# A vision tower on one core: GLA operands zeroed earlier and two tiles' products moved, shared-expert units of 144 and 384 columns, expert routing issued in three pieces

## What is computed

```python
h = _L0_tok_ref(L0_tok_log_dt, L0_tok_Lambda, x, 512)
h = jnp.concatenate([jnp.broadcast_to(cls_tok, (h.shape[0], 1, h.shape[2])), h], axis=1)
h = h + _L0_attn_ref(_layernorm(h), ...)   # gated linear scans, both directions
h = h + _L0_ffn_ref(_layernorm(h), ...)    # 8 experts, top 2, F = 256; shared expert, 512 wide
h = h + _L1_attn_ref(_layernorm(h), ...)   # GLA
h = h + _L1_ffn_ref(_layernorm(h), ...)    # 8 experts, top 2, F = 352; shared expert, 1408 wide
```

```python
q = silu(x @ Wq.T) * SCALE;  k = sigmoid(x @ Wk.T);  g = log_sigmoid(-k)
S = exp(g_t)[:, :, None] * S + k_t[:, :, None] * v_t[:, None, :];  o_t = q_t @ S     # v = x
go = o @ Wog.T + x @ Wig.T
out = o * rsqrt(mean(o*o) + EPS) * g_weight * go * sigmoid(go)
```

## Time and profile before

| | us |
|---|---|
| median of 3 runs (1746.93 to 1756.14) | 1748.59 |
| the profiled execution, its own time | 1747.31 |
| its span in the profile | 1745.5 |
| PE (TensorE) busy | 1483.2 (85%) |
| DVE (VectorE) busy | 795.7 (46%) |
| ACT (ScalarE) busy | 311.7 (18%) |
| mean granted TensorE clock | 0.956 of 2.4 GHz |

### The profile page before, as it was taken

The page is one execution under the profiler, slowest core; times in us unless marked ns, Lnnn a source line. Parts: engine busy times, 40 slices in busy tenths (PEclk is TensorE's granted clock), DMA queues, the critical chain, the costliest instruction groups (busy, mean ns, idle before and its releaser), DMA issues.

```text
span 1745.5 us, 19077 instructions
## 1 busy us (share of the span) xinstructions
PE 1483.2 (85%) x6021; PEld 1017.9 (58%) x6022; DVE 795.7 (46%) x1658; ACT 311.7 (18%) x575; POOL 381.1 (22%) x302
## 2 busy tenths in 40 slices
PE   0394748999899997259996899999999999999994
PEld 0393325888444443127775688888888755666652
DVE  7885487554222222832546655545555412222221
ACT  1022113211111111232222211111211111111110
POOL 0471320700244443001111160000000023333321
PEclk9999879999999999589998999999999999999997
DMA  2374005001855455300000611000000294333334
GB/s 50 67 127 101 0 24 200 20 31 49 310 94 96 84 85 107 115 1 0 1 1 25 227 32 37 18 18 18 18 29 8 88 357 77 61 65 66 66 60 121
DMA packets 73761, 128.86 MB, mean 74 GB/s; under 512 B 28784, under 2 KB 32752, under 8 KB 71280
## 3 DMA queue, kind: packets, MB, share of 16 engines
q1 hardware_dynamic: 53616, 86.20, 15.8%
q0 software_dynamic: 20096, 42.02, 13.3%
HBM read 81.86 MB, written 47.50 MB: 74 GB/s over the span
## 4 chain that ended last, share of the span: by engine, by line
PE 82%; DVE 10%; DMA 2%; issue 2%; ACT 1%; SPq 1%; POOL 0%; POOLq 0%; DVEq 0%; ACTq 0%
PE ps L1297 21%; PE ps L1234 11%; PE ps L1346 11%; PE ps L1363 10%; PE ps L1342 8%; PE ps L1707 6%; PE ps L402 3%; PE ps L1331 2%; DVE held L455 2%; PE ps L511 1%; DMA h_rows<-moe_scratch 1%; PE ps L1354 1%; PE ps L730 1%; PE ps L1679 1%; PE ps L731 1%
## 5 line engine op out<-in xcount | busy, mean ns | idle before, releaser
L1297 PE MATMUL ps<-moe_rounded 128*128 128x512 f32 (+1 forms) x1800 | 406.2, 369 | 0.0
L1297 PEld LDWEIGHTS ps<-moe_rounded 128*128 128x128 f32 x1800 | 316.1, 190 | 66.7
L1074 DVE SCALAR_TENSOR_TENSOR held<-ps,moe_scratch,held 128x512 f32<-128x512 f32 (+1 forms) x255 | 183.8, 746 | 221.9 <-PE ps L1234 221.9
L1234 PE MATMUL ps<-moe_rounded 128*128 128x512 f32 (+3 forms) x885 | 232.9, 392 | 16.3 <-DVE moe_rounded L1058 15.0
L1149 POOL DMA_INDIRECT moe_scratch<-xn_rows,moe_scratch x80 | 78.1, 976 | 597.0 <-PE ps L1331 584.7
L1346 PE MATMUL ps<-moe_experts,moe_scratch 128*128 x640 | 196.1, 460 | 1.3 <-ACT moe_scratch L1215 0.9
L1234 PEld LDWEIGHTS ps<-moe_rounded 128*128 128x128 f32 (+2 forms) x885 | 150.3, 172 | 64.9 <-DVE moe_rounded L1058 16.7
L1363 PE MATMUL ps<-moe_experts,moe_scratch 128*128 (+1 forms) x400 | 185.3, 594 | 2.6 <-DVE moe_scratch L1097 2.3
L1158 POOL DMA_INDIRECT h_rows<-moe_scratch x80 | 126.6, 1582 | 235.0 <-DVE moe_scratch L1090 158.3
L1084 DVE TENSOR_TENSOR moe_scratch<-moe_scratch,ps 128x256 f32<-128x256 f32 (+1 forms) x80 | 37.7, 471 | 275.6 <-ACT moe_scratch L1221 275.6
L1346 PEld LDWEIGHTS ps<-moe_experts,moe_scratch 128*128 128x128 f32 x640 | 118.7, 190 | 60.8 <-issue 1.8
(11 more groups left out here) (273 smaller groups left out, 1420.4 us busy)
## 6 DMA issues: line engine op xcount, KB each, us to landing
moe_experts<-in_ffn_gate_up SPq DMA_DIRECT2D x8, 1408.0 KB, 15.8
xn_rows<-moe_xn SPq DMA_DIRECT2D x2, 4096.0 KB, 13.2
moe_experts<-in_ffn_gate_up SPq DMA_DIRECT2D x8, 1024.0 KB, 12.3
moe_experts<-in_ffn_down SPq DMA_DIRECT2D x16, 512.0 KB, 14.4
h_rows<-held SPq DMA_DIRECT2D x8, 1024.0 KB, 4.1
moe_scratch<-in_ffn_sh_gate_up SPq DMA_DIRECT2D x15, 512.0 KB, 3.5
out<-h_rows SPq DMA_DIRECT2D x4, 1032.0 KB, 10.0
tokens<-sb SPq DMA_DIRECT2D x64, 64.0 KB, 2.3
```

The costliest lines, as they stand in the source:

```text
L1074: v.scalar_tensor_tensor(out=hb[0:rows, t, :], in0=ps[0:rows, 4 + r % 3, :], scalar=sg[0:rows, t:t + 1], in1=hb[0:rows, t, :], op0=ALU.mul ...
L1234: mm = t.matmul(out, lhs(k, x), rhs(k, y), start=(k == 0 and i == 0), stop=(k == ks - 1 and i == 2))
L1297: mm = t.matmul(unit_banks(unit)[j], weights(k, x, j), xT[y][:, k, unit_cols(unit)[0]], start=(k == 0 and i == 0), stop=(k == KD - 1 and i ...
```

## The change

It does five things.

1. Shared expert: unit 0 is the last 144 columns (tile 15 and the class tile), unit 4 is 384 columns (tiles 12 to 14). The downs of tiles 15 and 16 come with those of unit 1, as fifth and sixth in rank. So six downs stand in unit 2 and three (of unit 4) in the next block's unit 1.
2. Routing: VectorE enters the first block at once, and does the routing in three pieces: `segments` after the multiplication of unit 1, `slots_of` after the low part of unit 1, `tile_experts` after the first two adds. The third down of the first block waits for a new count, `RANKED`.
3. GLA: the zeroing stands before VectorE's first wait for `hb`.
4. GLA, VectorE: the low part of `xc3` before the split of the output weights; `low_part(0)` before the first operation of the decay chain, `low_part(1)` between scan and reciprocal, `cls_xw` behind the reciprocal. On ScalarE `high_part(1)` stands before `xw_out(0)`, and `xw_out(1)` before the copy of the class scores.
5. GLA, TensorE: `gate_x(0)`, `xw_of(1)` and `gate_x(1)` stand ahead of `attend(0)`, after `xw_of(0)`.

```diff
+RC = P + NB
...
-    hid, hidc = r.take(2, 2, QC), r.take(2, NB)
+    hid, hidc = r.take(2, 2, QC), r.take(2, RC)
...
+    DIFFERENCES, CHOICES, RANKED, ROUTED = 1, 2, 3, 4
...
-        return (slice(NCOL, NTOK), NB) if m == 0 else (slice((m - 1) * QC, m * QC), QC)
+        if m == 0:
+            return slice(NTOK - RC, NTOK)
+        return slice((m - 1) * QC, min(m * QC, NTOK - RC))
...
-        tiles = list(range(4 * (m - 1), 4 * m)) + ([NB] if m == 1 else [])
+        tiles = list(range(4 * (m - 1), min(4 * m, NB - 1))) + ([NB - 1, NB] if m == 1 else [])
...
-        return 4 if tile == NB else tile + (tile > 3)
+        return tile - NB + 5 if tile >= NB - 1 else tile + 2 * (tile > 3)
...
         if m == 0:
-            return ps[:, 7, 0:NB], ps[:, 7, NB:2 * NB]
-        p = 2 * ((m - 1) % 2)
-        return ps[:, p, :], ps[:, p + 1, :]
+            return ps[:, 7, 0:RC], ps[:, 7, RC:2 * RC]
+        p, w = 2 * ((m - 1) % 2), unit_width(m)
+        return ps[:, p, 0:w], ps[:, p + 1, 0:w]
+
+    def unit_width(m):
+        return unit_cols(m).stop - unit_cols(m).start
...
-        for j, oh in enumerate((oh0, oh1)):
...
-        c.link(v.tensor_tensor(cmp, bc(iot.unsqueeze(2), 2, NE), bc(incl.unsqueeze(1), 1, NTILE), ALU.is_ge))
-        c.link(v.tensor_reduce(etab, cmp, AX.X, ALU.add))
-        v.tensor_scalar(eti, etab, float(NE - 1), None, ALU.min).then_inc(rt, 1)
-        norm.closed(c)
-        v.wait_ge(sgm, 2)
+
+        def segments():
+
+            c.link(v.memset(anew, 1.0))
+            c.put(v.memset(anew[:, :, 0], 0.0))
+            c.link(v.memset(one8, 1.0))
+            v.wait_ge(rp, T + 1)
+            c.link(v.tensor_tensor_scan(upto.rearrange("p e t -> p (e t)"), anew.rearrange("p e t -> p (e t)"), ps[:, 6, 256:256 + T * NE], 0.0, ALU.mult, ALU.add))
+            c.link(v.tensor_scalar(cni, upto[:, :, T - 1], float(P - 1), None, ALU.add))
+            c.link(v.tensor_tensor(upto, upto, in_tile, ALU.subtract))
+            v.tensor_tensor(mm8, ps[:, 6, 64:64 + T * NE].rearrange("p (t e) -> p t e", e=NE), upto.rearrange("p e t -> p t e"), ALU.add).then_inc(rt, 1)
+            c.link(v.tensor_scalar(cni, cni, 7, None, ALU.arith_shift_right))
+            c.link(v.tensor_copy(cnt, cni))
+            c.link(v.tensor_tensor_scan(incl, one8, cnt, 0.0, ALU.mult, ALU.add))
+
...
+            c.link(v.tensor_tensor(base, incl, cnt, ALU.subtract))
+            c.link(v.tensor_scalar(base, base, float(P), None, ALU.mult))
+            v.wait_ge(rt, RANKED)
+            c.link(v.tensor_tensor(mm8, mm8, bc(base.unsqueeze(1), 1, T), ALU.add))
+            for j, oh in enumerate((oh0, oh1)):
+                c.link(v.tensor_tensor(t8, oh, mm8, ALU.mult))
+                c.link(v.tensor_reduce(m1, t8, AX.X, ALU.add))
+                c.link(v.tensor_copy(slot_u[:, j], m1))
...
+            v.wait_ge(sgm, 2)
+
+        def tile_experts():
+
+            c.link(v.tensor_tensor(cmp, bc(iot.unsqueeze(2), 2, NE), bc(incl.unsqueeze(1), 1, NTILE), ALU.is_ge))
+            c.link(v.tensor_reduce(etab, cmp, AX.X, ALU.add))
+            v.tensor_scalar(eti, etab, float(NE - 1), None, ALU.min).then_inc(rt, 1)
+            norm.closed(c)
...
+        ROUTING = {("mul", 1): segments, ("lo", 1): slots_of, ("early", 1): tile_experts}
...
+                if is_first(b) and (what, m) in ROUTING:
+                    ROUTING[what, m]()
...
-                        s.wait_ge(dn, b * T + (unit_rank(unit_tiles(m - 2)[3]) + 1 if m >= 3 else (5 - T, 13 - T, 0)[m]))
+                        s.wait_ge(dn, b * T + (unit_rank(unit_tiles(m - 2)[3]) + 1 if m >= 3 else (6 - T, 14 - T, 0)[m]))
...
-            m = 0 if tile == NB else tile // 4 + 1
-            j = 0 if tile == NB else tile % 4
+            m, j = (0, tile - NB + 1) if tile >= NB - 1 else (tile // 4 + 1, tile % 4)
...
+            if is_first(b) and r == 2:
+                t.wait_ge(rt, RANKED)
             if r >= 3:
                 t.wait_ge(acc, b * T + r - 2)
...
+        c.put(v.memset(ss, 1.0))
+        c.link(v.memset(bv, 0.0))
+        c.put(v.memset(bv[:, :, 0], 1.0))
+        c.put(v.memset(kcz, 0.0))
+        c.put(v.memset(own, 0.0))
+        v.memset(xc3[0:ROWS3].bitcast(F32), 0.0).then_inc(c3, 1)
+        v.memset(xwc3[0:ROWS3].bitcast(F32), 0.0).then_inc(c3, 1)
+        c.wait()
+        for j in range(3):
+            c.put(v.tensor_copy(own[KH * j:KH * j + NB], ident[KH * j:KH * j + NB, KH * j:KH * j + NB]))
         for tiles in GROUPS:
             for n in tiles:
...
-        c.put(v.memset(ss, 1.0))
-        c.link(v.memset(bv, 0.0))
...
+        v.wait_ge(c3, 4)
+        v.tensor_tensor(xc3[KH:KH + NB], xn[0:NB, NB, :], xc3[0:NB], ALU.subtract).then_inc(c3, 1)
         v.wait_ge(wsp, 2)
         for w, to in ((wog, wo), (wig, wi)):
             v.tensor_tensor(to[:, 1], w, to[:, 0], ALU.subtract).then_inc(wsp, 1)
-        v.wait_ge(c3, 4)
-        v.wait_ge(xr, 1)
-        v.tensor_tensor(xc3[KH:KH + NB], xn[0:NB, NB, :], xc3[0:NB], ALU.subtract).then_inc(c3, 1)
...
+        low_part(0)
         v.wait_ge(bnd, 4 * NG + 1)
         v.scalar_tensor_tensor(out=qr, in0=qr, scalar=SILU_SCALE, in1=sq, op0=ALU.mult, op1=ALU.mult).then_inc(qkr, 1)
...
         c.link(v.tensor_tensor_scan(F(pv), F(av), F(bv), 0.0, ALU.mult, ALU.add))
+        low_part(1)
         c.link(v.reciprocal(F(av), F(pv)))
+        cls_xw()
         v.wait_ge(qkr, 1)
         v.tensor_tensor(qr, qr, pv, ALU.mult).then_inc(qkr, 1)
...
-        low_part(0)
-        cls_xw()
-        low_part(1)
...
         high_part(0)
+        high_part(1)
         xw_out(0)
-        high_part(1)
+        xw_out(1)
...
-            if j + 1 < T:
+            if 1 <= j and j + 1 < T:
                 xw_out(j + 1)
...
         xw_of(0)
+        gate_x(0)
+        xw_of(1)
+        gate_x(1)
         attend(0)
         cls_scores()
...
-            gate_x(j)
-            if j + 1 < T:
+            if j >= 2:
+                gate_x(j)
+            if 1 <= j and j + 1 < T:
                 xw_of(j + 1)
             outs(j)
```

More of the change, by code:

```diff
@@ L882, in sync @@
         for q in range(NQ):
-            sp.wait_ge(acc, (NSH - 1) * T + unit_rank(4 * q + 3) + 1)
+            sp.wait_ge(acc, (NSH - 1) * T + max(unit_rank(t) for t in range(4 * q, 4 * q + 4)) + 1)
             sp.dma_start(hd_rows[1:SEQ, 4 * q:4 * q + 4], hb[:, 4 * q:4 * q + 4, :]).then_inc(hst, 16)
@@ L1027, in vector @@
[L1027 to L1033, removed]
-        c.link(v.tensor_tensor(mm8, ps[:, 6, 64:64 + T * NE].rearrange("p (t e) -> p t e", e=NE), upto.rearrange("p e t -> p t e"), ALU.add))
@@ L1296, in block @@
                             for unit in units:
-                                mm = t.matmul(unit_banks(unit)[j], weights(k, x, j), xT[y][:, k, unit_cols(unit)[0]],
+                                mm = t.matmul(unit_banks(unit)[j], weights(k, x, j), xT[y][:, k, unit_cols(unit)],
                                               start=(k == 0 and i == 0), stop=(k == KD - 1 and i == 2))
@@ L1458, in vector @@
         v.wait_ge(xr, 1)
-        c.put(v.memset(ss, 1.0))
-        c.link(v.memset(bv, 0.0))
-        c.put(v.memset(bv[:, :, 0], 1.0))
-        c.put(v.memset(kcz, 0.0))
-        c.put(v.memset(own, 0.0))
-        v.memset(xc3[0:ROWS3].bitcast(F32), 0.0).then_inc(c3, 1)
-        v.memset(xwc3[0:ROWS3].bitcast(F32), 0.0).then_inc(c3, 1)
-        c.wait()
-        for j in range(3):
-            c.put(v.tensor_copy(own[KH * j:KH * j + NB], ident[KH * j:KH * j + NB, KH * j:KH * j + NB]))
+        v.wait_ge(c3, 4)
+        v.tensor_tensor(xc3[KH:KH + NB], xn[0:NB, NB, :], xc3[0:NB], ALU.subtract).then_inc(c3, 1)
         v.wait_ge(wsp, 2)
@@ L1471, in vector, with low_part, cls_xw @@
             v.tensor_tensor(to[:, 1], w, to[:, 0], ALU.subtract).then_inc(wsp, 1)
-        v.wait_ge(c3, 4)
-        v.wait_ge(xr, 1)
-        v.tensor_tensor(xc3[KH:KH + NB], xn[0:NB, NB, :], xc3[0:NB], ALU.subtract).then_inc(c3, 1)
+        def low_part(j):
+            n = ORDER[j]
+            r = rows_of(n)
+            v.wait_ge(tev, T + j + 1)
+            v.tensor_tensor(xT[:, j % 2, 1, :, 0:r], ps[:, TB2[j % 2], 0:KD * r].rearrange("p (k n) -> p k n", k=KD),
+                            xT[:, j % 2, 0, :, 0:r], ALU.subtract).then_inc(xl, 1)
+        def cls_xw():
+            v.wait_ge(xwr, 1)
+            v.wait_ge(c3, 7)
+            v.tensor_tensor(xwc3[KH:KH + NB], ps[0:NB, XW_BANK, :], xwc3[0:NB], ALU.subtract).then_inc(c3, 1)
+        low_part(0)
         v.wait_ge(bnd, 4 * NG + 1)
@@ L1525, in cls_attention @@
             v.tensor_tensor(atcF[0:ROWS3].rearrange("p (q b) n -> p q b n", b=NG), spread, mine, ALU.mult).then_inc(atcr, 1)
-        def cls_xw():
-            v.wait_ge(xwr, 1)
-            v.wait_ge(c3, 7)
-            v.tensor_tensor(xwc3[KH:KH + NB], ps[0:NB, XW_BANK, :], xwc3[0:NB], ALU.subtract).then_inc(c3, 1)
         def gated(j):
```

33 lines of the change are left out of this document (9 added, 24 removed).

## The result

Four runs of the changed kernel have a median of 1695.4 us (1692.52 to 1697.31), against 1750.59 us (four runs) of the kernel before, measured with it: ratio 0.9681, 95% interval 0.9649 to 0.9713. The profiled execution took 1694.29 us, its span is 1692.5 us, 53.0 shorter than before, at a mean granted clock of 0.966. The page of the changed kernel shows where TensorE's time went: the products of gate and up at L1317 (L1297 before, 406.2 us busy), the down products at L1254 (L1234, 16.3 us of idle before) and the GLA products at L1728 (L1707, 11.9 us).

The account below looks back on a forecast made before the run. TensorE, last-ending chain for 82% of the span, was taken as the bound. 13.8 + 11.6 + 11.0 + 16.2 = 52.6 us off the profiled 1747.3 gives 1694.7, as median 1696; range 1683 to 1722.

Parts of the forecast that it names:

- zeroing first: GLA: zeroing moves under VectorE's idle before its first load; TensorE projects at 723.9 instead of 737.70; gain 13.8 us.
- products in the decay chain: GLA: 48 products move ahead of `attend(0)`; `outs(1)` starts 14.6 us earlier, less 3.0 for the clock; gain 11.6.
- routing in pieces and units: Shared expert: routing in pieces, 11.0 us, and units of 144 and 384 columns, 16.2 us.
- of it, routing: First block of each layer: unit 3 starts at 305.3 instead of 310.09, one more down done; 5.5 us, twice, 11.0.
- of it, units: Shared expert: 384-column products save 19.2 us, narrow ones stay at 0.111, a 0.2 stop per block costs 3.0; gain 16.2.
- the stop at the sixth down: First block: TensorE's sixth down waits 1.9 us for the third add, behind `tile_experts` and unit 2's multiplication.
- the 13.58 us of idle: GLA: VectorE stood 13.58 us before its first load; zeroing under it costs nothing, 2.6 us without that cover.
- a clock that falls under these products: GLA: 24 products with 16 weight columns stand ahead of a 1.4 us stop; 3.0 us taken off for half clock.
- The wait until 784.1: GLA: TensorE waits until about 784.1 because `masked(1)` stands on VectorE behind the class attention.
- Rival 1: GLA: the decay chain edit gives nothing, low parts lengthen the chain by 2.2 us; 1710 us, chance 0.10.
- The repeated stop in unit 2: Shared expert, each block: the sixth down waits 0.2 us for the third add; 3.0 us in all.
- Rivals 2, 3 and 4: Narrow products: load plus columns, 0.176 (1719 us, chance 0.06); plain fp32 pace, 0.245 (1744, 0.13); both, 0.356 (1784, 0.05).

Follow-up runs that it names:

- zeroing only: The kernel before with only the GLA zeroing (seven memsets, three copies) moved ahead of the loads: 1780.43 us on chip 8, ratio 0.9942 to the kernel before.
- products back: The changed kernel with the first tiles' low parts (except that of `xc3`) and products put back behind the decay chain: 1757.88 us on chip 8.
- units back: The changed kernel with units of 16 and 512 columns and the ranks of before: 1761.11 us on chip 8, ratio 0.9849 to the kernel before.
- the repeat: The changed kernel again, unaltered, on chip 9: 1743.62 us, ratio 0.9711 to the kernel before.
- routing whole: The changed kernel with the routing's vector work in one piece ahead of the first block, as before: 1746.91 us on chip 8, ratio 0.9759 to the kernel before.

## Why the prediction was right

The forecast was 1696 us, the median is 1695.4. The table takes this apart; its third column compares the two first traces, its fourth is explained below it.

| step | forecast | measured, first chip | from the experiments |
|---|---|---|---|
| zeroing first | 13.8 (12 to 15) | 14.0 | 14.3 |
| products in the decay chain | 11.6 (8 to 15) | 11.8 | 12.5 |
| routing in pieces and units | 27.2 (20 to 31) | 27.2 | |
| of it, routing | 11.0 (7 to 12) | 11.3 | 14.7 |
| of it, units | 16.2 (13 to 19) | 15.9 | 12.5 |
| sum | 52.6 | 53.0 | |

The last column has 14.3 from zeroing only and 12.5 from products back, each by its stage; the 14.7 is from the run with units back, and the last 12.5 is 27.2 less 14.7 and no run's own.

The 27.2 are 10.68 in the first layer and 53.0 less 36.5 in the second. How they split depends on whose the stop at the sixth down is. I charged it to the routing. Measured that way, unit 3 starts 5.12 and 4.77 us sooner after its layer's first product, and the extra down adds 0.69 to each: 11.3. With the units of before there is no such stop: first blocks of 43.08 and 42.76 became 35.57 in the run with units back, 14.7 together, and the units' share is then 12.5, just below my bounds of 13 to 19, as 14.7 is above those of 7 to 12 for the routing. Only the sum of the two is free of this choice.

*Zeroing*: right in cost, place and size; the reading of the 13.58 us of idle as cover was all it needed.

*Decay chain*: right in the mechanism, in part lucky in the size. The start of `xw_of(0)`, forecast at 766.1 in old times, came at 766.4, and the 48 products took the place of the wait. But I took 3.0 off for a clock that falls under these products. It stayed full over them, also over the 24 with 16 weight columns, and fell only behind the short `attend` and `outs(0)` work. The wait until 784.1 that I had forecast for `masked(1)` isn't there either. From `xw_of(0)` to `outs(1)` I had 21.7 us without the clock, and it took 24.10: the two errors left 2.4 where I had 3.0. Rival 1 falls.

*Routing*: the first down was not late in the first layer and 0.17 in the second (I had 0.35), the fourth 0.22 (0.6), the sixth 1.35 (1.9); the granted clock was 1.00, as forecast.

*Units*: narrow products at 0.111, as taken, which is the step that mattered; unit 4 at 0.176 (0.179), some 1.3 us more saved in all (my 24 x 15 x 0.053 is 19.1, not 19.2). The repeated stop in unit 2 is 0.2: in the second layer's block above the four downs 1030.84 to 1033.78 take 2.94, against 2.76. Unforeseen was the 0.14 at unit 4's first down, in one layer only, which took about as much back. Rivals 2, 3 and 4 fall by the 5.49 us of 16 pairs. The row shows 0.111 for 144 columns and 0.119 for 256. The Trainium skill's page "TensorE: Matmul & The Clock Gate", Part 3, by which a load overlaps only a matmul of another row group, is contradicted here at each width: by it, load and columns would add up.

On chips 8 to 10 the forecast would have been wrong by 48 us in level, but not in difference: there the change gave 1791.6 less 1743.6, 48.0 us.

## What to carry to other kernels

Where a narrow and a wide product alternate, ask what the narrow one costs beyond its weight load: up to 256 columns were nearly free here (0.0075 us for the last 112), so columns belong in it rather than in a product that is bound by its columns. Beyond that they would cost what they cost in a wide product, by the numbers above; no run tried it. An engine's idle time ahead of its first load is the cheapest place for set-up work that anything later waits for. When vector work is cut into pieces, put the pieces where that engine stands idle, and earlier rather than later; each must end before the next low part or add that TensorE is due to need, and what waits for the last piece (here the scatters) moves with it.

## What the runs showed that I had not expected

The same program took 1695.4 us on one chip and 1743.6 on another. Of the 48.2 us, 23.8 and 24.0 lie in each layer's second block, in which most of GpSimd's scatters run. On the first chip the same scatters run beside a block of 35.70 us at full clock, as its windows show.

```profile
320.20:355.90 35.70, 35.70 (x172) 29.59 (x171) 18.88 (x29) 6.56 (x12) 23.24 (x24) 1.00 0.14 39
```

The first block of the changed kernel, with the first 13 of the 34 scatters beside it, is not slower on either. That is a matter of when they start: in the repeat TensorE's first such stop comes 24 us after the layer's first scatter, at 328.4 after 304.6. Where more of the scatters lie in the first layer's first block, it is stalled too: 51.82 us with the routing whole (27 of them) and 55.73 with zeroing only (30), against 43.08 for the kernel before on the first chip. All traces of chips 8 to 10 have such stops, and none of the first two. Whether the chip makes the difference or something else that changed between the first measurement and these was not separated, and the cause stays open.
